# Two rank products per image pair, narrower Q passes, and the second norm's row fields moved from GpSimd to VectorE and ScalarE

## What is computed

```python
h = concat(tok(x), txt)                         # (64, 114, 256)
n = layernorm(h)
Q, K, V = elu(n @ Wq.T + bq) + 1, elu(n @ Wk.T + bk) + 1, n @ Wv.T + bv      # 16 heads of 16
h = h + ((Q @ (K.T @ V)) / (Q . sum(K) + 1e-6)) @ Wo.T + bo
x = layernorm(h); logits = x @ gate_w.T         # 8 experts, the best one is taken
xs = x * sigmoid(max(logits))                   # of the tokens of expert e
h = h + ((xs @ w_up[e].T) * silu(xs @ w_gate[e].T)) @ w_down[e].T
```

## Time and profile before

| | before |
|---|---|
| median of 3 runs | 432.34 us (431.60 to 432.51) |
| profiled execution | 431.59 us, its span 429.8 us |
| busy TensorE, VectorE, ScalarE, GpSimd | 95%, 82%, 70%, 73% |
| mean granted TensorE clock | 0.98 of 2.4 GHz |
| chain that ended last | TensorE 83%, GpSimd 5%, issue 4%, VectorE 3%, ScalarE 2% |

### The profile page before, as it was taken

The page is one execution under the profiler, slowest core; times in us unless marked ns, Lnnn a source line. Parts: engine busy times, 40 slices in busy tenths (PEclk is TensorE's granted clock), DMA queues, the critical chain, the costliest instruction groups (busy, mean ns, idle before and its releaser), DMA issues.

```text
span 429.8 us, 13564 instructions
## 1 busy us (share of the span) xinstructions
PE 406.6 (95%) x4389; PEld 399.4 (93%) x4389; DVE 352.1 (82%) x1140; ACT 298.8 (70%) x760; POOL 312.0 (73%) x699
## 2 busy tenths in 40 slices
PE   8999999999999999999999999999988999999940
PEld 7999899999999999999999999999887999999940
DVE  5678568999999999999999999998796887777840
ACT  5444477688778778878877877886684777777720
POOL 4065213688888888888888888888867777777772
PEclk9999999999999999999999999999998999999995
DMA  8965111333322231331121112100683589422220
GB/s 299 353 207 165 51 48 47 99 98 87 111 90 64 64 100 39 92 116 44 38 64 51 39 54 60 54 25 24 182 229 104 183 243 283 164 86 88 75 92 14
DMA packets 34152, 46.49 MB, mean 108 GB/s; under 512 B 8843, under 2 KB 25857, under 8 KB 34083
## 3 DMA queue, kind: packets, MB, share of 16 engines
q1 hardware_dynamic: 24860, 30.50, 23.5%
q0 software_dynamic: 9216, 15.12, 11.2%
q10 hardware_dynamic: 6, 0.00, 0.0%
HBM read 26.87 MB, written 17.17 MB: 102 GB/s over the span
## 4 chain that ended last, share of the span: by engine, by line
PE 83%; POOL 5%; issue 4%; DVE 3%; ACT 2%; DMA 1%; POOLq 0%; SPq 0%; DVEq 0%; ACTq 0%
PE b_kg L1491 8%; PE b_kg L1492 8%; PE b_kg L1493 8%; PE b_w L1491 8%; PE b_w L1492 7%; PE b_w L1493 7%; PE b_att L1606 6%; PE b_t L1556 3%; PE b_v L1493 3%; PE b_v L1491 3%; PE b_v L1492 3%; PE b_t L1620 3%; PE b_att L1543 3%; PE b_att L1491 3%; PE b_att L1493 2%
## 5 line engine op out<-in xcount | busy, mean ns | idle before, releaser
L705 POOL DMA_INDIRECT sorted_rows<-rows,place x64 | 75.4, 1177 | 20.3 <-issue 9.4
L831 POOL DMA_INDIRECT out<-result,rows_all x64 | 66.9, 1045 | 19.5 <-issue 12.8
L937 ACT ACTIVATE q_exp<-b_w,bq_s 128x228 f32<-128x228 f32 x64 | 28.9, 451 | 24.0 <-PE b_w L1493 23.9
L1491 PE MATMUL b_w<-xnT_hi,wq_hi 128*128 128x264 f32 x128 | 39.6, 309 | 0.2
L1491 PE MATMUL b_kg<-wkgv_hi,xnT_hi 128*114 128x264 f32 x128 | 38.7, 302 | 0.4 <-DVE patch_out L1128 0.4
L1040 ACT ACTIVATE silu_g<-b_kg,rows_all 128x128 f32<-128x128 f32 x64 | 23.5, 368 | 21.8 <-PE b_kg L1493 19.6
L1491 PE MATMUL b_kg<-wgu_hi,xsT_hi 128*128 x128 | 37.2, 290 | 0.0
L1492 PE MATMUL b_w<-xnT_lo,wq_hi 128*128 128x264 f32 x128 | 36.5, 285 | 0.0
L1492 PE MATMUL b_kg<-wkgv_lo,xnT_hi 128*114 128x264 f32 x128 | 36.5, 285 | 0.0
L1492 PE MATMUL b_kg<-wgu_lo,xsT_hi 128*128 x128 | 36.4, 285 | 0.0
L1493 PE MATMUL b_kg<-wkgv_hi,xnT_lo 128*114 128x264 f32 x128 | 36.4, 284 | 0.0
(11 more groups left out here) (252 smaller groups left out, 1647.4 us busy)
## 6 DMA issues: line engine op xcount, KB each, us to landing
rows_all<-sorted_rows SPq DMA_DIRECT2D x64, 130.0 KB, 3.3
rows_all<-in_x SPq DMA_DIRECT2D x18, 384.0 KB, 4.3
rows_all<-in_txt SPq DMA_DIRECT2D x32, 154.0 KB
rows_all<-in_wgu_in SPq DMA_DIRECT2D x8, 256.0 KB, 3.0
rows_all<-patch_out SPq DMA_DIRECT2D x48, 36.0 KB
sorted_rows<-tail_rows SPq DMA_DIRECT2D x9, 130.0 KB
sorted_rows<-rows,place POOLq DMA_INDIRECT x64, 3.7
rows_all<-in_wdown_in SPq DMA_DIRECT2D x2, 512.0 KB, 4.2
```

The costliest lines, as they stand in the source:

```text
L705: G.indirect_dma_start(out=scratch[0:EXPERTS * REGION, :], out_offset=bass.IndirectOffsetOnAxis(ap=place[:, k, b:b + 1], axis=0), in_=rows ...
L831: G.indirect_dma_start(out=out, out_offset=bass.IndirectOffsetOnAxis(ap=rows_all[:, t.n, ID:ID + 1].bitcast(I32), axis=0), in_=result[:, k ...
L937: S.activation(q_exp[:, c, :], at, ACT.Exp, bias=bq_s[:, c:c + 1])
L1491: T.matmul(to, left_hi, right_hi, start=start, stop=False, skip_group_check=seeded)
```

## The change

- **TensorE.** `rank(p)` has two products: the tokens earlier in the image, and `so_far`, whose two halves are now the counts before the first and before the second image. It waits for the first half of `count_chosen(p)` (the counts before image 2), where it waited for `count_chosen(p-1)`. Of the twelve passes of `queries`, ten have 256 columns instead of 264; the first pass into either bank keeps 264. `early_count` and `late_count` halve their products.
- **GpSimd.** `rstd2_of` loses the negated mean and the copy of the mean into the row, and makes half the scale. `scatter` loses four instructions: the token's number is copied by `ids_in` ahead of it, the gain comes from ScalarE, the place from VectorE. `count_chosen` has two additions instead of one, the second behind the first, and stands behind `scatter` and ahead of `rstd1_of` and `top_value`. At the end of the pairs the stores of duo 0 come before `count_chosen(31)` and `scatter(30)`, those of duo 1 before `scatter(31)`.
- **ScalarE.** `means(p)` (one instruction, behind `tanh`) negates the mean, `gains(p)` (two instructions, behind `keys`) writes the gain. `centred` waits for `means` and no longer for GpSimd. At the end of the pairs they are spread by hand, and each `tanh` stands ahead of a `gate_and_up`.
- **VectorE.** `stats_2` writes mean and variance straight into the row. `places` is a product over 16 columns and, behind a wait for it, a sum that writes whole numbers; it was a product with a running sum for each image.

The diff, less declarations, the changed counts of the waits in `stats_1`, `stats_2` and `route`, and the two counting functions:

```diff
@@ -658,24 +657,21 @@
         k = p % 4
         pool.wait_ge(mv2_ready, p + 1)
         if p >= 1:
-            pool.wait_ge(rstd2_step, 5 * p)
-        if p >= 1:
+            pool.wait_ge(rstd2_step, 3 * p)
             pool.wait_ge(top_n_ready, p)
         if p >= 4:
-            pool.wait_ge(centred_ready, p - 3)
-        G.tensor_scalar(ve2[:], mv2[:, k, :, 1], LN_EPS, None, ALU.add).then_inc(rstd2_step, 1)
-        G.tensor_scalar(mean_neg[:, k, :], mv2[:, k, :, 0], -1.0, None, ALU.mult).then_inc(rstd2_step, 1)
-        pool.wait_ge(rstd2_step, 5 * p + 1)
-        G.tensor_tensor(rstd2[:, k, :], ve2[:], half_neg[0:TOK, :], ALU.pow).then_inc(rstd2_step, 1)
-        pool.wait_ge(rstd2_step, 5 * p + 3)
-        G.tensor_copy(rows[:, k, :, MEAN], mv2[:, k, :, 0]).then_inc(rstd2_step, 1)
+            pool.wait_ge(gain_ready, p - 3)
+        G.tensor_scalar(ve2[:], rows[:, k, :, GAIN], LN_EPS, 4.0, ALU.add, ALU.mult).then_inc(rstd2_step, 1)
+        pool.wait_ge(rstd2_step, 3 * p + 1)
+        G.tensor_tensor(rstd2_half[:, k, :], ve2[:], half_neg[0:TOK, :], ALU.pow).then_inc(rstd2_step, 1)
+        pool.wait_ge(rstd2_step, 3 * p + 2)
         pool.wait_ge(rstd1_step, 5 * p + 5)
-        G.tensor_tensor(ratio[:], spread1[:, p % 8, :], rstd2[:, k, :], ALU.mult).then_inc(rstd2_step, 1)
+        G.tensor_tensor(ratio[:], spread1[:, p % 8, :], rstd2_half[:, k, :], ALU.mult).then_inc(rstd2_step, 1)
     def top_value(p):
         pool.wait_ge(top_ready, p + 1)
-        pool.wait_ge(rstd2_step, 5 * p + 5)
+        pool.wait_ge(rstd2_step, 3 * p + 3)
         if p >= 2:
             pool.wait_ge(tanh_ready, p - 1)
         G.tensor_tensor(top_n[:, p % 2, :], top[:, p % 2, :], ratio[:], ALU.mult).then_inc(top_n_ready, 1)
@@ -684,23 +680,26 @@
         pool.wait_ge(chosen_ready, p + 1)
         if p >= 1:
+            pool.wait_ge(so_far_ready, 2 * p)
             pool.wait_ge(rank_done, p)
-            pool.wait_ge(so_far_ready, p)
-        G.tensor_tensor(so_far[0:TOK, (p + 1) % 2], so_far[0:TOK, p % 2], chosen[:, p % 2],
-                        ALU.add).then_inc(so_far_ready, 1)
+        now, then = so_far[0:TOK, p % 2], so_far[0:TOK, (p + 1) % 2]
+        G.tensor_tensor(now[:, 1], now[:, 0], chosen[:, p % 2, 0], ALU.add).then_inc(so_far_ready, 1)
+        pool.wait_ge(so_far_ready, 2 * p + 1)
+        G.tensor_tensor(then[:, 0], now[:, 1], chosen[:, p % 2, 1], ALU.add).then_inc(so_far_ready, 1)
+    def ids_in(p):
+        if p >= 4:
+            pool.wait_ge(scattered[p % 4], 32 * (p // 4))
+        G.tensor_copy(rows[:, p % 4, :, ID].bitcast(I32), ids_s[:, 2 * p:2 * p + 2]).then_inc(id_ready, 1)
     def scatter(p):
         k = p % 4
-        pool.wait_ge(tanh_ready, p + 1)
+        pool.wait_ge(gain_ready, p + 1)
         pool.wait_ge(centred_ready, p + 1)
-        G.tensor_scalar(route_w[:], tanh_top[:, p % 2, :], 1.0, 0.5, ALU.add, ALU.mult).then_inc(field_step, 1)
-        G.tensor_copy(rows[:, k, :, ID].bitcast(I32), ids_s[:, 2 * p:2 * p + 2]).then_inc(field_step, 1)
-        pool.wait_ge(field_step, 4 * p + 1)
-        G.tensor_tensor(rows[:, k, :, GAIN], route_w[:], rstd2[:, k, :], ALU.mult).then_inc(field_step, 1)
         pool.wait_ge(place_ready, p + 1)
-        G.tensor_copy(place[:, k, :], place_f[:, k, :]).then_inc(field_step, 1)
-        pool.wait_ge(field_step, 4 * p + 4)
+        pool.wait_ge(id_ready, p + 1)
         for b in range(2):
             G.indirect_dma_start(
                 out=scratch[0:EXPERTS * REGION, :],
@@ -747,20 +746,23 @@
         G.tensor_copy(slot_expert[:, 0:EARLY_TILES], past[:, :, 0]).then_inc(early_ready, 1)
     def step(i):
+        if i == EARLY_PAIRS + 7:
+            early_rows()
         if 0 <= i - 3:
             rstd2_of(i - 3)
+            ids_in(i - 3)
         if 0 <= i - 4:
             scatter(i - 4)
+        if 0 <= i - 3:
+            count_chosen(i - 3)
         if 0 <= i + 2 < PAIRS:
             rstd1_of(i + 2)
         if 0 <= i - 3:
             top_value(i - 3)
-            count_chosen(i - 3)
         if i == EARLY_PAIRS + 5:
             early_past()
         if i == EARLY_PAIRS + 6:
             early_sums()
-            early_rows()
         if i in GU_SPLIT_STEPS:
             gate_up_low(GU_SPLIT_STEPS.index(i))
         if i in DOWN_SPLIT_STEPS:
@@ -812,28 +814,31 @@
     pool.wait_ge(patches_ready, PT)
     for i in range(PAIRS + 1):
         step(i)
+    def store(m):
+        for t in tiles_of(m):
+            k = t.slot(RESULT_RING)
+            pool.wait_ge(result_ready, t.n + 1)
+            G.indirect_dma_start(
+                out=out, out_offset=bass.IndirectOffsetOnAxis(ap=rows_all[:, t.n, ID:ID + 1].bitcast(I32), axis=0),
+                in_=result[:, k, :], in_offset=None,
+                bounds_check=TOKENS - 1, oob_is_err=False).then_inc(stored[k], 16)
     count_chosen(PAIRS - 2)
     scatter(PAIRS - 3)
     rstd2_of(PAIRS - 2)
+    ids_in(PAIRS - 2)
     top_value(PAIRS - 2)
+    store(Turn(0, 0))
+    count_chosen(PAIRS - 1)
     scatter(PAIRS - 2)
-    count_chosen(PAIRS - 1)
     rstd2_of(PAIRS - 1)
+    ids_in(PAIRS - 1)
     top_value(PAIRS - 1)
+    store(Turn(0, 1))
     scatter(PAIRS - 1)
-    def duo_step(j):
-        if (j - 1).within(DUOS):
-            m = j - 1
-            for t in tiles_of(m):
-                k = t.slot(RESULT_RING)
-                pool.wait_ge(result_ready, t.n + 1)
-                G.indirect_dma_start(
-                    out=out, out_offset=bass.IndirectOffsetOnAxis(ap=rows_all[:, t.n, ID:ID + 1].bitcast(I32), axis=0),
-                    in_=result[:, k, :], in_offset=None,
-                    bounds_check=TOKENS - 1, oob_is_err=False).then_inc(stored[k], 16)
-    straight(range(1, DUOS + 1), duo_step)
+    for m in range(2, DUOS):
+        store(Turn(0, m))
 @block.scalar
@@ -872,15 +877,30 @@
         act.wait_ge(top_n_ready, p + 1)
         if p >= 2:
-            act.wait_ge(field_step, 4 * (p - 1))
-        S.activation(tanh_top[:, p % 2, :], top_n[:, p % 2, :], ACT.Tanh, scale=0.5).then_inc(tanh_ready, 1)
+            act.wait_ge(gain_ready, p - 1)
+        S.activation(tanh_top[:, p % 2, :], top_n[:, p % 2, :], ACT.Tanh).then_inc(tanh_ready, 1)
+    def gains(p):
+        act.wait_ge(tanh_ready, p + 1)
+        for b in range(2):
+            half = rstd2_half[:, p % 4, b:b + 1]
+            last = S.activation(rows[:, p % 4, b, GAIN:GAIN + 1], tanh_top[:, p % 2, b:b + 1], ACT.Identity, bias=half, scale=half)
+        last.then_inc(gain_ready, 1)
+    def means(p):
+        act.wait_ge(mv2_ready, p + 1)
+        if p >= 1:
+            act.wait_ge(centred_ready, p)
+        S.activation(mean_neg[:], rows[:, p % 4, :, MEAN], ACT.Copy, scale=-1.0).then_inc(mean_neg_ready, 1)
     def centred(p):
-        act.wait_ge(rstd2_step, 5 * p + 2)
+        act.wait_ge(mean_neg_ready, p + 1)
         for b in range(2):
             last = S.activation(rows[:, p % 4, b, 0:D], rows[:, p % 4, b, 0:D], ACT.Identity,
-                                bias=mean_neg[:, p % 4, b:b + 1])
+                                bias=mean_neg[:, b:b + 1])
         last.then_inc(centred_ready, 1)
     def normalised(p):
@@ -955,8 +975,12 @@
             seed_bias(i - 2)
         if 0 <= i - 4:
             tanh(i - 4)
+        if 0 <= i - 3:
+            means(i - 3)
         if 0 <= i:
             keys(i)
+        if 0 <= i - 4:
+            gains(i - 4)
         if 0 <= i + 1 < PAIRS:
             normalised(i + 1)
         if 0 <= i:
@@ -1057,25 +1081,35 @@
     seed_bias(PAIRS - 2)
     rows_high(Turn(0, 0))
     tanh(PAIRS - 4)
+    means(PAIRS - 3)
+    gains(PAIRS - 4)
     denominators(PAIRS - 1)
     S.activation(silu_ahead[:], bq_s[:, 0:1], ACT.Silu)
     centred(PAIRS - 3)
     rows_high(Turn(0, 1))
     attention_high(PAIRS - 1)
+    tanh(PAIRS - 3)
     gate_and_up(Turn(0, 0))
+    gains(PAIRS - 3)
     rows_high(Turn(0, 2))
-    tanh(PAIRS - 3)
     act_high(Turn(0, 0))
     gate_and_up(Turn(0, 1))
+    means(PAIRS - 2)
+    centred(PAIRS - 2)
     rows_high(Turn(0, 3))
-    centred(PAIRS - 2)
     tanh(PAIRS - 2)
     act_high(Turn(0, 1))
     gate_and_up(Turn(0, 2))
+    gains(PAIRS - 2)
+    means(PAIRS - 1)
+    centred(PAIRS - 1)
     rows_high(Turn(0, 4))
-    centred(PAIRS - 1)
     tanh(PAIRS - 1)
-    straight(STEPS_B, duo_step)
+    gate_and_up(Turn(0, 3))
+    act_high(Turn(0, 2))
+    rows_high(Turn(0, 5))
+    gains(PAIRS - 1)
+    straight(range(DRAIN_DUOS + 1, DUOS + 1), duo_step)
 @block.vector
@@ -1266,11 +1301,10 @@
             dve.wait_ge(place_ready, p)
         if p == PAIRS - 2:
             dve.wait_ge(wo_done, PAIRS)
-        for b in range(2):
-            last = V.tensor_tensor_reduce(place_e[:, b, :], rank_bank(p)[:, b * EXPERTS:(b + 1) * EXPERTS],
-                                          chosen[:, p % 2, b, :], 1.0, 0.0, ALU.mult, ALU.add,
-                                          place_f[:, p % 4, b:b + 1])
-        last.then_inc(place_ready, 1)
```

(21 more changed lines are left out.)

40 lines of the change are left out of this document (17 added, 23 removed).

## The result

The changed kernel takes **434.31 us** (median of 5, 434.05 to 435.45) against 432.31 (median of 5) for the kernel before: ratio 1.0063, 95% interval 1.0041 to 1.0084. It is **slower by 0.6%**, where 429.3 and "faster" were forecast.

A forecast was written before the change was run, and what follows sets the result against it. A closed loop of Q passes, ScalarE and VectorE bounds the pairs, GpSimd's store lag the end. -1.0 + 0.9 - 0.3 - 2.6 = -3.0 us gives 428.6 against the profiled execution, median 429.3, range 427.2 to 431.8.

The forecast's parts named there:

- Q passes: TensorE in the pairs: ten of 32 x 12 passes get 8 columns less, 0.033 us per step, -1.0 us.
- Rank: TensorE in the pairs: two of four products go; worth 0 in the steps, about -0.1 for each of the last four pairs.
- rival A: TensorE is the bound in the pairs, so rank counts too: 3.2 us more, 426.1; chance 0.05.
- Places: VectorE's new pair of instructions takes 0.28 us (0.25 to 0.65); hidden in the steps, +0.1 in the drain.
- Rival E: VectorE's second chain takes over in the pairs if places is slow: up to +4, 433.3; chance 0.07 with other delays.
- ScalarE: Three more small instructions per step, taken as 0.45 us; each later result has over 1 us until its reader: 0.
- the loop: In the pairs, Q passes, ScalarE, VectorE, Q passes form a closed loop of one step's length without slack.
- Step 30: TensorE waits 2.0 us ahead of rank(27) for the count behind scatter(26); net +0.9 us (0 to +1.7).
- Rival D: A new TensorE wait of 2.0 us may drop the clock, costing half of 3.4: 431.0; chance 0.12.
- Drain: End of the pairs: -0.1 x 4 for rank, +0.1 for VectorE's chain, together -0.3 us.
- Stores: Four GpSimd stores ahead of scatter(31) let the lag behind results shrink from 3.2 to 0.4 us: -2.6.
- Rival C: The stores' lag is held at 1.66 us or more: 430.4, or 431.9 at 3.2; chance 0.18.

The follow-up runs named there:

- q_alone: Kernel before with only the Q-pass part: ten of the twelve Q passes have 256 columns; 430.26 us, ratio 0.997.
- gains_first: Changed kernel, but ScalarE writes the gains ahead of keys in every step; 432.07 us, ratio 1.0015.
- fill_wait: Changed kernel, but TensorE does 56 unread products of ones while it waits ahead of rank(27); 432.35 us, ratio 1.0035.
- tanh_late: Changed kernel, but ScalarE's tanh(31) stands behind gate_and_up(3) and act_high(2); 432.17 us, ratio 1.0023.
- combo_b: Changed kernel with count_first and gains_first, and rstd2_of(31), ids_in(31) and top_value(31) ahead of scatter(30); 426.63 us, ratio 0.9885.
- fields_alone: Kernel before with only mean, scale and place moved to ScalarE and VectorE, with ScalarE's new order; 432.28 us, ratio 1.0018.
- stores_back: Changed kernel, but the four stores of duos 0 and 1 stand behind scatter(31) again; 434.23 us, ratio 1.0072.
- count_first: Changed kernel, but in step 30 alone GpSimd counts pair 27 ahead of scatter(26); 429.46 us, ratio 0.9948.
- rank_undone: Changed kernel without the rank part: four products, one count per pair at its old place behind top_n; 428.89 us, ratio 0.9936.
- combo_a: Changed kernel with count_first, gains_first and tanh_late together; 427.15 us, ratio 0.9897.
- combo_c: combo_b with act_u reading the up half from PSUM, one instruction per tile; 426.31 us, ratio 0.9874.
- act_psum: Changed kernel, but act_u reads the up half from PSUM, one instruction per tile, and ScalarE writes no up_g; 433.03 us, ratio 1.0035.
- rank_alone: Kernel before with only the rank part: two products and a count per image, directly behind scatter; 445.58 us, ratio 1.0337.

## Why the prediction was wrong

- **Q passes**, -1.0: right (-0.8 in the steps, -1.1 in the sum of q_alone). That the steps fell to 8.19 and not to 8.22 is the rank part.
- **Rank**, 0 in the steps: nearly right; 0.7 us over all steps. The 0.04 us that TensorE was said to have in hand aren't there in the kernel before. Of rival A's 3.2 us this is a fifth.
- **Places** were hidden, and took 0.37 us (0.16 + 0.17 with a gap of 0.04) for 0.28 assumed, inside the bounds. Rival E didn't happen.
- **ScalarE**, three instructions for 0: the sizes were in the range (`means` 0.09 and `gains` 0.56 from start to next start, 0.65 for 0.45 assumed), and the loop didn't notice. But the text listed who is queued behind `gains` and not what waits for it at its end: `scatter`, and with it GpSimd's whole round.
- **Step 30**, +0.9: **the step that failed**. It measured +4.6. The mechanism, rank(27) behind `scatter(26)`, was named, its size was not. Forecast was the count 3.54 us behind the start of Q(30), measured were 4.67 (303.82 + 0.20 - 299.35, where Q(30) now starts). 0.92 of the difference is the assumed "backlog of the steps before gone": `rstd2_of(27)` was to start 1.18 ahead of Q(30), and started 0.26 ahead (before: 0.43), because `scatter` waits for `gains` in each step and GpSimd can't catch up. gains_first shows that: with the gains ahead of keys it starts 1.44 ahead, and TensorE waits 1.92 us, the 2.0 of the forecast. The other 0.2 lies between `rstd2_of(27)` and the count, where 0.64 us of idle time stand ahead of the DMA (0.33 before); that isn't the gains, which were written by 296.75, and its cause is open. So TensorE waited 3.10, not 2.0. And the clock: the sum had nothing for it. Rival D stood at 0.12 and priced the fall at 1.7, which fits a fall of 3.4 us (1.4 to 1.6 measured); here it lasted 6.8 us, and fill_wait gives 2.5 for it. So +4.6 is the forecast 0.9, some 1.1 of longer wait, 2.5 of clock, and a remainder of 0.1.
- **Drain**, -0.3: wrong sign, +1.6. The text let the tanh of pair 31 come 0.9 later "in front of `gate_and_up(3)`" with 1.0 us of cover. It came 1.9 us later (24.84 behind Q(31), 22.93 before), since the two early stores stand ahead of `top_n(31)`, and ScalarE waited 3.85 us for it. tanh_late (-1.3) and combo_b show it. 1.05 of the 1.6 go with the rank part, which was to bring 0.4 here. The first duos were counted as gaining time for the stores, not as losing it to them.
- **Stores**, -2.6: -1.3. Rival C: the lag went from 3.16 to 1.66 and was held. Even the free lag is 0.80, not 0.4, so -2.2 would have been the most (tanh_late: 4.64 from last result to last store). The text had nothing for ScalarE's new order, with which the stores at their old place stand at 4.44 us (fields_alone, stores_back).
- With Q passes and the rest of the steps -2.0, step 30 +4.6, first duos +1.6, duos -0.1 and stores -1.3 the sum is +2.8 us, against +2.0 in the medians. The traced execution of the changed kernel is its slowest, with the long fall of the clock.

## What to carry over

When a wait is added, compute when its releaser arrives from who the *releaser* waits for now, not from how much work it lost: an engine relieved of work only comes earlier if its own inputs do. Work put early into a queue (the four stores) must be priced by everything queued behind it on that engine, down to the engine that waits for the last of these. And parts of a change are not a sum: rank alone cost 14 us, with the fields moved it cost 5 to 6, with one count ahead of `scatter` nothing that can be told from noise (count_first against rank_undone: 364.69 and 364.75 in the sums, 429.46 and 428.89 us).

## What the hardware showed that was not expected

- A store is held by VectorE's product of two SBUF operands for a definite time. In the changed kernel 24 of the 64 stores had `act_u` running 0.125 us after their start, and each of these was longer than 0.972 us by what `act_u` still had to run, within 6 ns (0.227 for 0.228, 0.136 for 0.137). One more was held, the store of tile 8, whose `act_u` started 0.128 us behind it; it was longer by 0.41, nearly the whole of `act_u` (0.40):

```profile
350.24 1.39 POOL L822 DMA_INDIRECT out<-result,rows_all  x1 [0.66 <-DVE result L1425]
```

Near the start of a store the rule isn't sharp: with `act_u` 0.030 us ahead of the store in count_first and 0.029 behind it in stores_back the store wasn't held, with 0.038 behind it in combo_a it was, by 0.33. What decides there is open. Products that read one operand from PSUM (`result`, and `act_u` in combo_c) held none; with `result` at that point, 81 times in all traces, no store but those that `act_u` met was longer by more than 0.03 us. Three stores of the first duos were longer by 0.08 to 0.16 us with no `act_u` at that point; why isn't shown. The Trainium skill, SBUF — State Buffer, "Who interferes with whom", says that a VectorE instruction with two SBUF inputs contends with a GpSimd instruction that reads SBUF, which agrees; its inference there, that the making of descriptors is spared, does not hold for these stores.
- From this the stores' lag behind the results has steps: 0.80, 1.66, 3.16 and 4.44 us in these kernels. Single stores can move it by a step: in the changed kernel it stood at 0.80 at tile 8, and the held store of that tile (0.41 longer), with the next results only 2.05 us behind, brought it to 1.72 at tile 10. In count_first it slipped from 1.66 to 0.80, from the one store of tile 18 on that wasn't held.
- Behind TensorE's wait ahead of rank(27) the granted clock stayed at 2.4 GHz when it was 1.92 us (gains_first) and fell to 1.2 GHz when it was 3.1 us (changed, stores_back, tanh_late, act_psum: for 3.4 or 6.8 us) or 3.77 us (rank_alone: 6.8 us). With TensorE kept busy by idle products of ones through the same wait it did not fall. But the length of a wait does not decide alone. In the first duos of every kernel TensorE waits 2.05 to 2.20 us ahead of the same product; in 11 of the 16 traces the clock fell within 1.7 us of its end, for 3.4 us, and in five it did not. And in the changed kernel it stayed up behind 3.14 us without work (TensorE's timeline and the window behind):

```profile
338.89 0.38 PE L1525 MATMUL b_kg<-wgu_hi,xsT_hi 128*128 x1 [3.14 <-ACT up_g L1065]
```

```profile
338.89:346.00 7.11, 7.11 (x61) 6.92 (x62) 6.25 (x20) 5.63 (x19) 5.58 (x6) 1.00 0.52 151
```
